# A two-layer cross-attention and expert kernel: the experts' first product goes from one float32 pass to three float32r passes

## The reference, cut to what matters

```
scores = jax.nn.softmax(xf @ gate_w.T, axis=-1)
vals, idx = jax.lax.top_k(scores.T, k)            # k = 224 tokens for each of 8 experts
y = layernorm(xf[flat_idx].reshape(k, n, d)) * ln_w + ln_b
h = jnp.einsum('knd,nfd->knf', y, fc1s) + b1s     # first product, 256 -> 1024
h = jax.nn.gelu(h, approximate=True)
out = jnp.einsum('knf,ndf->knd', h, fc2s) + b2s   # second product, 1024 -> 256
xf = xf.at[flat_idx].add(out * kept_w[..., None])
```

## Time and profile before

| | us |
|---|---|
| median of 3 runs | 723.4 (722.26 to 724.54) |
| the profiled execution, its own time | 720.77 |
| its span in the trace | 719.0 |
| PE busy / PEld busy | 680.2 / 572.6 |
| DVE / ACT / POOL busy | 519.2 / 358.8 / 333.9 |

### The profile page before, as it was taken

The page is one execution under the profiler, slowest core; times in us unless marked ns, Lnnn a source line. Parts: engine busy times, 40 slices in busy tenths (PEclk is TensorE's granted clock), DMA queues, the critical chain, the costliest instruction groups (busy, mean ns, idle before and its releaser), DMA issues.

```text
span 719.0 us, 16447 instructions
## 1 busy us (share of the span) xinstructions
PE 680.2 (95%) x6471; PEld 572.6 (80%) x6471; DVE 519.2 (72%) x1166; ACT 358.8 (50%) x700; POOL 333.9 (46%) x232
## 2 busy tenths in 40 slices
PE   7889999999999999999898999999997999999998
PEld 4677788875568999999786777777665887999998
DVE  5787888887867454431767888888889785848464
ACT  2221222215864655655567877877877353232323
POOL 2332433426975578774336778788786000000000
PEclk9999999999999999999999999999999999999999
DMA  9979100003863487797464886778640000000000
GB/s 283 336 252 87 36 26 26 27 26 85 219 211 109 132 221 208 197 204 118 112 154 94 182 172 166 173 153 182 137 95 2 3 2 14 1 27 1 26 14 27
DMA packets 67677, 81.57 MB, mean 113 GB/s; under 512 B 32931, under 2 KB 56067, under 8 KB 65267
## 3 DMA queue, kind: packets, MB, share of 16 engines
q1 hardware_dynamic: 64210, 72.68, 41.4%
q0 software_dynamic: 2816, 3.67, 2.8%
q10 hardware_dynamic: 576, 4.19, 1.4%
HBM read 60.45 MB, written 19.31 MB: 111 GB/s over the span
## 4 chain that ended last, share of the span: by engine, by line
PE 64%; DVE 10%; ACT 10%; issue 6%; DMA 5%; POOL 4%; SPq 0%; DVEq 0%; POOLq 0%; ACTq 0%
PE psum L2577 6%; PE psum L900 5%; PE psum L1282 5%; ACT probs L1974 5%; PE psum L1740 5%; PE psum L207 4%; PE psum L366 4%; PE psum L1299 4%; PE psum L2271 3%; PE psum L2258 3%; DMA sum_d<-outs,idx 3%; PE psum L2230 3%; PE psum L2296 2%; PE psum L936 2%; ACT qpk L1964 2%
## 5 line engine op out<-in xcount | busy, mean ns | idle before, releaser
L2065 DVE TENSOR_REDUCE mx<-psum 112x2 f32<-112x750 f32 x128 | 113.2, 926 | 8.0 <-PE psum L2230 7.6
L1974 ACT ACTIVATE probs<-psum 125x448 f32<-125x448 f32 x192 | 91.0, 559 | 16.6 <-PE psum L2258 16.0
L1881 POOL TENSOR_TENSOR half_sum<-probs 125x896 f32<-125x896 f32 x30 | 62.5, 2082 | 28.8 <-ACT probs L1974 28.8
L900 PE MATMUL psum<-w_parts,c_parts 128*125 128x512 f32 x282 | 71.2, 403 | 3.7 <-DVE kv L656 3.5
L900 PEld LDWEIGHTS psum<-w_parts,c_parts 128*125 128x125 f32 x282 | 51.4, 186 | 18.0 <-DVE kv L656 3.7
L2230 PE MATMUL psum<-kpk,qpk 96*128 96x375 bf16 x256 | 62.3, 325 | 2.3 <-DVE mx L2065 2.2
L2258 PE MATMUL psum<-qpk,kpk 128*128 128x112 bf16 x768 | 60.5, 213 | 4.3 <-ACT probs L1974 4.2
L2258 PEld LDWEIGHTS psum<-qpk,kpk 128*128 128x128 bf16 x768 | 45.5, 98 | 23.3 <-issue 7.2
L1887 POOL TENSOR_TENSOR tile_sum<-half_sum,probs 125x896 f32<-125x896 f32 x30 | 62.9, 2096 | 2.4
L1582 ACT ACTIVATE ctx_all<-psum,cols 128x448 f32<-128x448 f32 (+1 forms) x40 | 22.4, 561 | 80.8 <-PE psum L1748 80.8
L1554 POOL TENSOR_TENSOR rs<-ve,mhalf 112x4 f32<-112x4 f32 (+1 forms) x5 | 4.4, 886 | 106.5 <-DVE ve L1597 106.5
(11 more groups left out here) (259 smaller groups left out, 1638.8 us busy)
## 6 DMA issues: line engine op xcount, KB each, us to landing
we<-in_we SPq DMA_DIRECT2D x12, 1024.0 KB, 5.3
kparts_d<-kp SPq DMA_DIRECT2D x16, 562.5 KB, 4.9
kpk<-kparts_d SPq DMA_DIRECT2D x32, 281.2 KB, 4.4
ctx_all<-in_ctxT SPq DMA_DIRECT2D x16, 375.0 KB, 4.1
kpk<-kparts_d SPq DMA_DIRECT2D x32, 187.5 KB, 4.9
we<-in_we ACTq DMA_DIRECT2D x4, 1024.0 KB, 13.2
kpk<-kparts_d SPq DMA_DIRECT2D x32, 93.8 KB, 4.1
qparts_d<-qp SPq DMA_DIRECT2D x16, 168.0 KB, 3.2
```

The costliest lines, as they stand in the source:

```text
L900: ins = pe.matmul(banks[B_KV[t]][0:KT, :], parts_of[:, x, k, t * KT:(t + 1) * KT], w_parts[:, k, w], start=(k == 0 and (x, w) == SPLIT[0]) ...
L1881: pool.tensor_tensor(half_sum[:, m], probs[:, m, 0], probs[:, m, 1], ALU.add)\
L1974: act.activation(probs[:, m, t, g * HU * SQ:(g + 1) * HU * SQ], banks[B_ST[u % 3]][0:KT, 0:HU * SQ], ACT.Exp, scale=SCALE)\
L2065: dve.tensor_reduce(mx[:, n % 2, MAX_AT + 2 * j:MAX_AT + 2 * j + 2], psum[0:SQ, first:first + 2, 0:SK], AX.X, ALU.max)\
```

## The change

The first product takes the three passes of the second. ScalarE makes `rT[:, 0]` and the new buffer `we1_high` (one slot, in the place of buffers `z` and `total` of the stage before, two halves of 1024 columns); VectorE makes the remainders `rT[:, 1]` and `we1_low`, and those of chunks 0 and 1 of the second weights (`OWN_CHUNKS = 2` of 8); GpSimd makes the other six after VectorE. The rows `rT` have one slot now, so `turned` waits for the first product before it. The keys of batch 0 are loaded one DMA per step behind the second weights; those of batch 1 after `x_all` is loaded; those of batch 2 after the queries of batches 0 and 1.

```diff
-    rT = sb(ctx, "rT", [128, 2, KC, CAP])
+    rT = sb(ctx, "rT", [128, 2, KC, CAP], F32R)
...
-        with sp.Fori(0, E0 // 2 - 1) as i:
...
-        for b in range(AHEAD):
-            for r in (3, 2, 1):
-                for m in range(KC):
-                    load_keys(sp, b, r, m)
+        first_keys = [(r, m) for r in (3, 2, 1) for m in range(KC)]
+        for e in range(E0 - 2):
+            s = e % 2
+            sp.wait_ge(fc1_ps.sem, fc1_ps.at(e))
+            sp.dma_start(we[:, s, 0:KC * F0], ...)
+            sp.wait_ge(fc2_ps.sem, fc2_ps.at(e))
+            sp.dma_start(we[:, s, KC * F0:], ...)
+            load_keys(sp, 0, *first_keys[e])
...
         def turned(e):
             act.wait_ge(rT_ps.sem, rT_ps.at(e))
+            if e:
+                act.wait_ge(fc1_ps.sem, fc1_ps.at(e - 1))
+        def round_first_weights(e, i, s):
+            act.wait_ge(w1_in[s].sem, w1_in[s].at(i))
+            if e:
+                act.wait_ge(fc1_ps.sem, fc1_ps.at(e - 1))
+            for h in range(2):
+                half = slice(h * F0 // 2, (h + 1) * F0 // 2)
+                act.activation(we1_high[:, :, half], we1[:, s, :, half], ACT.Copy).then_inc(we1_split.sem, 1)
...
                 turned(e + 1)
+                round_first_weights(e + 1, i + s, 1 - s)
                 round_weights(e + 1, i + s, 1 - s)
...
         for b in range(3):
             keep_value(act, b, 0)
+        act.wait_ge(z_out.sem, z_out.at(PAIRS - 1))
+        act.wait_ge(total_out.sem, total_out.at(PAIRS - 1))
+        round_first_weights(0, 0, 0)
         keep_value(act, 3, 0)
...
         def rest_of_weights(e):
-            pool.wait_ge(we2_split.sem, we2_split.at(e, 1))
-            pool.tensor_tensor(we2_low[:, e % 2], ...)
+            pool.wait_ge(we2_split.sem, we2_split.at(e, 2))
+            others = slice(OWN_CHUNKS, FC)
+            pool.tensor_tensor(we2_low[:, e % 2, others], ...)
...
         split_tokens(1, slice(2, E0))
+        rest_of_first_weights(0)
+        rest_of_second_weights(0)
         dve.wait_ge(token_split.sem, token_split.at(5))
         one_hots(1, 0)
+        rest_of_rows(0)
...
             rest_of_hidden(e // 2, e % 2)
             if e + 2 < E0:
                 find((e + 2) // 2, e % 2)
+            if e + 1 < E0:
+                rest_of_rows(e + 1)
             if e + 3 < E0:
                 one_hots((e + 3) // 2, (e + 3) % 2)
+            if e + 1 < E0:
+                rest_of_first_weights(e + 1)
+                rest_of_second_weights(e + 1)
...
             finish(e // 2, e % 2)
...
-            pe.wait_ge(w1_in[s].sem, w1_in[s].at(i))
             pe.wait_ge(rT_done.sem, rT_done.at(e))
             for f in range(FC):
                 g = f // 2
+                if f % (FC // 2) == 0:
+                    pe.wait_ge(we1_split.sem, we1_split.at(e, f // (FC // 2) + 3))
...
                 for k in range(KC):
+                    for w, x in SPLIT:
+                        ins = pe.matmul(..., we1_low[:, s, k, chunk] if w else we1_high[:, k, chunk], rT[:, x, k], ...)
...
+        sp.wait_ge(x2_in[-1].sem, x2_in[-1].at(0))
+        for r in (3, 2, 1):
+            for m in range(KC):
+                load_keys(sp, 1, r, m)
         for b in range(2):
             store(b)
         for b in range(2):
             load_queries(b)
+        for r in (3, 2, 1):
+            for m in range(KC):
+                load_keys(sp, 2, r, m)
```

More of the change, by code:

```diff
@@ L184, in two_layer_kernel @@
     we1 = we[:, :, 0:KC * F0].rearrange("p s (k f) -> p s k f", k=KC)
+    we1_low = we_low[:, :, 0:KC * F0].rearrange("p s (k f) -> p s k f", k=KC)
     we2 = we[:, :, KC * F0:].rearrange("p s (f o) -> p s f o", f=FC)
@@ L189, in two_layer_kernel @@
     tables = [(before, "c_before"), (ones, "c_ones"), (token5, "c_token")]
+    with ExitStack() as over_z:
+        we1_high = sb(over_z, "we1_high", [128, KC, F0], F32R)
     z = sb(early, "z", [SQ, 2, D])
@@ L286, in two_layer_kernel @@
     ctx = ExitStack()
+    sb(ctx, "under_we1_high", [128, KC * F0 - 4 * D])
     iota = sb(ctx, "iota", [SQ, CAP], BF16)
@@ L1045, in two_layer_kernel @@
     rT_ps = sem(ctx, "rT_ps")
-    rT_done = sem(ctx, "rT_done")
+    rT_done = sem(ctx, "rT_done", 2)
+    we1_split = w_split.behind(w_split.at(0), 4)
     first_gelu = sb(ctx, "first_gelu", [1, 1])
@@ L1050, in two_layer_kernel @@
     h_low_done = sem(ctx, "h_low_done", FC // 2)
-    we2_split = sem(ctx, "we2_split", 2)
+    we2_split = sem(ctx, "we2_split", 3)
+    OWN_CHUNKS = 2
     fc2_ps = sem(ctx, "fc2_ps")
@@ L1064, in _ @@
         sp.dma_start(b2[:], d["b2"]).then_inc(tabs_in.sem, 16)
-        with sp.Fori(0, E0 // 2 - 1) as i:
[L1066 to L1070, removed]
-        for b in range(AHEAD):
-            for r in (3, 2, 1):
-                for m in range(KC):
-                    load_keys(sp, b, r, m)
+        first_keys = [(r, m) for r in (3, 2, 1) for m in range(KC)]
+        for e in range(E0 - 2):
+            s = e % 2
+            sp.wait_ge(fc1_ps.sem, fc1_ps.at(e))
+            sp.dma_start(we[:, s, 0:KC * F0], d["we"][e + 2, :, 0:KC * F0]).then_inc(w1_in[s].sem, 16)
+            sp.wait_ge(fc2_ps.sem, fc2_ps.at(e))
+            sp.dma_start(we[:, s, KC * F0:], d["we"][e + 2, :, KC * F0:]).then_inc(w2_in[s].sem, 16)
+            load_keys(sp, 0, *first_keys[e])
     @block.scalar
@@ L1141, in rest_of_weights @@
         def rest_of_weights(e):
[L1142 to L1144 removed]
+            pool.wait_ge(we2_split.sem, we2_split.at(e, 2))
+            others = slice(OWN_CHUNKS, FC)
+            pool.tensor_tensor(we2_low[:, e % 2, others], we2[:, e % 2, others],
+                               we2_high[:, e % 2, others].bitcast(F32), ALU.subtract).then_inc(we2_split.sem, 1)
         pool.wait_ge(z_out.sem, z_out.at(PAIRS - 1))
@@ L1213, in find, with rest_of_rows, rest_of_first_weights, rest_of_second_weights @@
             dve.wait_ge(found_all.sem, found_all.count())
+        def rest_of_rows(e):
+            dve.wait_ge(rT_done.sem, rT_done.at(e, 1))
+            dve.tensor_tensor(rT[:, 1], banks[B_RT][:, 0:KC * CAP].rearrange("p (k c) -> p k c", k=KC),
+                              rT[:, 0].bitcast(F32), ALU.subtract).then_inc(rT_done.sem, 1)
+        def rest_of_first_weights(e):
+            s = e % 2
+            for h in range(2):
+                half = slice(h * F0 // 2, (h + 1) * F0 // 2)
+                dve.wait_ge(we1_split.sem, we1_split.at(e, 2))
+                dve.tensor_tensor(we1_low[:, s, :, half], we1[:, s, :, half], we1_high[:, :, half].bitcast(F32),
+                                  ALU.subtract).then_inc(we1_split.sem, 1)
+        def rest_of_second_weights(e):
+            own = slice(0, OWN_CHUNKS)
+            dve.wait_ge(we2_split.sem, we2_split.at(e, 1))
+            dve.tensor_tensor(we2_low[:, e % 2, own], we2[:, e % 2, own], we2_high[:, e % 2, own].bitcast(F32),
+                              ALU.subtract).then_inc(we2_split.sem, 1)
         def rest_of_hidden(i, s):
@@ L1281, in step @@
                 for k in range(KC):
-                    ins = pe.matmul(banks[B_F[g]][:, (f % 2) * CAP:(f % 2 + 1) * CAP],
-                                    we1[:, s, k, f * 128:(f + 1) * 128], rT[:, s, k],
-                                    start=(k == 0), stop=(k == KC - 1))
+                    for w, x in SPLIT:
+                        chunk = slice(f * 128, (f + 1) * 128)
+                        ins = pe.matmul(banks[B_F[g]][:, (f % 2) * CAP:(f % 2 + 1) * CAP],
+                                        we1_low[:, s, k, chunk] if w else we1_high[:, k, chunk], rT[:, x, k],
+                                        start=(k == 0 and (w, x) == SPLIT[0]),
+                                        stop=(k == KC - 1 and (w, x) == SPLIT[-1]))
                 if f % 2:
```

2 lines of the change are left out of this document (1 added, 1 removed).

## The result

The changed kernel takes 723.9 us (median of 20 runs, 717.85 to 731.62) against 718.48 us for the kernel before (20 runs, 714.49 to 725.13, measured beside it): a ratio of 1.0062, 95% interval 1.0037 to 1.0087. The ratio leaves out the two slowest executions of the changed kernel (729.5 and 731.62 us), which ran in a slower state of the chip, at a lower granted clock. It says 4.5 us slower (2.7 to 6.3) where 3 us faster was forecast. The profiled execution took 720.88 us with a span of 719.1. That is as long as the profiled execution before (720.77), but what lies ahead of the change happened to be 4.35 us shorter in it.

What follows compares the result with a forecast made beforehand. TensorE was taken to bound the expert block (12.55 us a step), then the additions into `sum_d`. Terms +2.85 + 1.7 - 4.3 - 1.5 - 1.7 = -2.95 gave 717.8 us profiled, 720.4 median, range 715.5 to 725.5.

Steps and rivals of the forecast that it cites:

- GpSimd: Expert steps: its smaller remainder ends 5.1 us into the next step, needed at 6.1; costs nothing, 1 us of cover.
- -4.3 of the experts: Expert steps: five with masks save 0.45 us each, the rest 0.69 each; 2.25 plus 2.07 us saved.
- Rival D: Expert steps: VectorE's remainders and GpSimd's gather block each other, 0.9 us a step, 4.5 more: 724.9; chance 0.14.
- Entry: Before step 0: masks and GpSimd's remainder exclude each other, TensorE starts at 235.2 instead of 232.37: +2.85 us.
- clock term of +1.7: At the entry: TensorE idle for 2.9 us, then 3.4 us at half rate; +1.7 us, bounds 0 and 3.4.
- Behind the experts: After the last step: last addition issued sooner, -1.5 us; TensorE's gap shrinks to 1.0 and the clock stays, -1.7.
- Keys: Spread key loads: slack beside the weights, later batches needed 20 us later; zero, bounds 0 and +1.5 us.
- A: Entry: no shut-out, both masks pass before GpSimd takes the memory; 4.55 us less, 715.9; chance 0.18.
- B: Entry: the shut-out stands but the clock does not fall; 1.7 us less, 718.7; chance 0.13.
- C: Behind the experts: additions hardly sooner (-0.5) and the clock falls there as before; 723.1; chance 0.15.
- Chances: Whole kernel: faster (below 721.2) 0.61, same 0.28, slower (above 725.6) 0.11; the forecast itself 0.40.
- The weighed rule: Entry and steps: first starter holds the SBUF port, masks still end at 234.5; descriptor generation unaffected, so VectorE-gather blocking gives nothing.

Runs made afterwards that it cites:

- masks_early: Changed kernel with each step's masks placed between its `h_low` instructions, all else as there; ratio 0.9952 to the kernel before, experts 95.70 us.
- reordered: Changed kernel with masks split between `h_low`, `find` before the last `h_low`, masks and rows' remainder earlier at the entry; ratios 0.9914 and 0.9887 to the kernel before.
- keys_only: Kernel before with only the diff's edits to the key loads; ratio 0.9982 to the kernel before, experts 99.60 us.
- find_early: Changed kernel with only `find` moved ahead of the step's last `h_low`; ratio 1.0026 to the kernel before, experts 100.67 us.
- extra_reads: Kernel before plus three unused VectorE instructions with two SBUF inputs behind each step's masks, 3.1 us; ratio 1.0113 to the kernel before.

## Why the prediction was wrong

**The step that failed** is *GpSimd*, in "The change, part by part": "Nothing, with 1 us of cover", on which the -4.3 of the experts rests. It counted when GpSimd's smaller remainder would be ready and kept the gathers at the length of before. The runs showed gathers of 3.55 to 4.57 us in three laps, and instead of 4.3 us less the experts took 3.55 more. The trace of before already showed what would happen: the gather of 280.27 in the earlier trace rows ends at 281.95, 0.92 behind the masks of the earlier trace rows (278.94 + 2.09 = 281.03). The same 0.9 appears in the changed kernel (0.88). A run longer by 3.1 us therefore meant a gather longer by up to 3.1 us: GpSimd saved 1.05 on its remainder and lost 1.9 to 2.9 on the two gathers in these laps. That sum stood in reach: the lap of 12.55 us, of which 1.48 are idle, is 11.4 with the usual 0.3 between issues; less 1.05, plus up to 3.1, it is 13.4 (measured 12.92), against 12.1 for TensorE and VectorE. The lap explains steps 4 and 5. The larger loss, in step 1, is the other consequence of the same shut-out: rows that land late, and the clock that falls behind the wait.

**Rival D** had the right pair of engines and the wrong loser. It let VectorE wait for the gather (0.9 us a step), with a chance of 0.14, since the masks kept their 2.09 beside gathers. They do, because it is the gather that waits. At the entry it is the other way round, VectorE waits for GpSimd's `tensor_tensor` (5.38 us for two masks).

**Experts, by size.** The waits for rows aside, the forecast held: the steps with masks that don't wait take 11.98 to 12.06 (12.05 to 12.15 forecast), the last two steps 11.40, 0.70 less than before (0.69 forecast). The excess over 12.06 lies in three steps: 5.81 in step 1 (3.66 of waiting, 2.15 more with the clock down) and 1.16 and 1.08 in steps 4 and 5 (waits of 1.12 and 1.11): 8.05 us. 103.14 less that is 95.09, 4.5 under before, where 4.3 was forecast. In `masks_early` and `reordered`, where the run is cut, steps take 11.87, the 11.86 that the forecast gave for TensorE as the bound.

**Entry.** +2.46 against +2.85, by the mechanism named: masks of 5.38 us around GpSimd's 3.43. The clock term of +1.7 was absent in this profile and present with 1.6 in `masks_early`, whose idle time is the same 2.51 us. Stretches of that kernel at the entry (its step 0 starts at 232.65):

```profile
229.00:232.60 3.60, 1.15 (x6) 0.62 (x4) 3.55 (x2) 0.81 (x1) 2.06 (x1) 1.00 0.56 173
232.60:236.20 3.60, 3.55 (x18) 3.58 (x19) 0.42 (x1) 0.85 (x3) 0.00 (x0) 0.56 0.27 82
```

So in these executions a gap of 2.5 us was a chance of losing 1.6, not a fixed price.

**Behind the experts** -3.33 against -3.2, by the mechanism named: the adds are over in time, TensorE's gap is 0.83 instead of 2.49, and the clock stays. **Keys** cost nothing in `keys_only`, as forecast; beside a late gather they probably cost something (step 1). That answers rivals A, B and C: the shut-out at the entry is real (not A), B's missing clock fall came true in this profile, C's gap did shrink. The forecast's -2.95 with 7.85 more for the experts and without the 1.7 would be +3.2, the profile shows +2.68, the runs +4.5 (2.7 to 6.3). Why the runs lie above the profile isn't settled. What follows the first scores takes 348.6 to 353.3 us in the profiles of these kernels, so one profile can't tell. That 723.9 lies inside the range given (715.5 to 725.5) is no support for the sum either: the range was built on a median of three runs, 723.4, and twenty runs of the same kernel have 718.48, so the forecast's 2.95 less would have been 715.5.

**Chances.** They don't follow as written. A quarter of the forecast (0.10), C (0.15) and half of D (0.07) are 0.32 for "same", where 0.28 stands, and D alone, at 724.9, lies below the 725.6 set for slower.

**The weighed rule.** The Trainium skill, SBUF — State Buffer, "Who interferes with whom", infers that a two-input `tensor_tensor` leaves descriptor generation alone. For the indirect gathers and additions here the measurement says otherwise: gathers of 1.0 us took up to 4.8, additions of 1.5 up to 5.1. The same section's general rule, that such an instruction contends with a GpSimd instruction that reads SBUF, agrees with these rows if the issue counts as one. That the one that starts first holds the port for its whole length falls short of them: the gather of 240.48 waited past the ends of three VectorE instructions (241.30, 242.44 and 243.57), until the run was over. That the reading of the row indices is what collides is possible and was not tested by itself.

## What to carry to other kernels

Before giving VectorE more instructions with two SBUF inputs, write down GpSimd's whole lap, and take every indirect DMA that could start inside the run to 0.9 us (a gather) or 1.4 us (an addition) behind the run's end. That is the worst case. If the lap then exceeds the step, cut the run with instructions that read PSUM: `masks_early`, which does this alone, brought 7.4 us in the experts against the changed kernel. Releasing GpSimd earlier brought 2.5 alone (`find_early`), and both together, with the entry's order, 9.0 (`reordered`). Where two engines are seen to touch in a trace, look at both lengths, and at the ends, to see who yields.

## What was not expected of the hardware

- An indirect DMA issue on GpSimd that starts inside the second or third of five back-to-back VectorE instructions with two SBUF inputs ends only 0.87 to 0.94 us (gather) or 1.35 to 1.38 us (addition) behind the fifth, after 3.5 to 5.1 us instead of 1.0 to 1.5.
- One that starts inside the first of them gets in behind it, with the run going on: the gather of 281.39 ends 0.92 behind the first mask. Two places don't fit this pattern: at the entry the gather of 221.68 ends 0.88 behind the last weights' remainder while masks follow, and in `extra_reads` an addition (307.13) gets in behind the second of three. What decides isn't settled.
- Memsets on VectorE (1.12 us for 1278 elements) don't touch it: the gather stays at 1.67, which it owes to the masks, and one that starts inside a memset takes 1.04.
- VectorE doesn't yield to a gather (two masks 2.08 to 2.10), but does to GpSimd's `tensor_tensor` (two masks 5.38 instead of 2.1).
- The same gap of 2.51 us on TensorE cost the clock in one kernel (0.56 over the next 3.6 us) and not in another (1.00 over the next 12).
